# Masks converted one pair after their load, and a first expert layer in fp16 parts

## What is computed

```python
# first attention: 16 heads of 64, mask (4, 1, 512, 512) in int32
energy = jnp.einsum('nqhd,nkhd->nhqk', Qh, Kh) * scale
energy = jnp.where(mask == 0, -1e20, energy)
attention = jax.nn.softmax(energy, axis=-1)
x = x + concat @ Wo
# first experts: 8 experts, each takes the 256 tokens of highest score out of 2048
y = _layernorm(xf[flat_idx].reshape(k, n, d), ln_gamma, ln_beta)
h = jax.nn.gelu(jnp.einsum('knd,nfd->knf', y, fc1s) + b1s, approximate=True)   # 256 -> 1024
o = jnp.einsum('knf,ndf->knd', h, fc2s) + b2s                                  # 1024 -> 256
out = xf.at[flat_idx].add((o * kept_w[:, :, None]).reshape(k * n, d))
```

## Time and profile before

| | |
|---|---|
| median of three runs | 1164.58 us (1164.51 to 1169.02) |
| profiled execution, time | 1166.58 us |
| profiled execution, span | 1164.8 us |
| PE busy | 1056.6 us (91%) |
| DVE, ACT, POOL busy | 753.1, 672.4, 555.8 us |
| first attention, from the first masked score to the last unit | 18 to 504 us |
| first experts | about 566 to 690 us |

### The profile page before, as it was taken

The page is one execution under the profiler, slowest core; times in us unless marked ns, Lnnn a source line. Parts: engine busy times, 40 slices in busy tenths (PEclk is TensorE's granted clock), DMA queues, the critical chain, the costliest instruction groups (busy, mean ns, idle before and its releaser), DMA issues. The chain is left out here.

```text
span 1164.8 us, 28791 instructions
## 1 busy us (share of the span) xinstructions
PE 1056.6 (91%) x10247; PEld 770.4 (66%) x10248; DVE 753.1 (65%) x2151; ACT 672.4 (58%) x1273; POOL 555.8 (48%) x685
## 2 busy tenths in 40 slices
PE   6998999999999999984799997698988867999996
PEld 3666677767777677674488884344554446888885
DVE  5886887788778877878411116677777774555553
ACT  5887876678668876856422235366766643343331
POOL 4677643656556653301436640666667523233312
PEclk9999999999999999995799999899999967999998
DMA  7533333333343334308646546424435231111110
GB/s 258 160 81 82 87 78 75 68 80 82 67 100 92 79 78 92 74 11 294 194 132 181 173 82 221 143 62 141 130 117 152 76 104 37 29 28 30 28 14 11
DMA packets 124380, 117.22 MB, mean 101 GB/s; under 512 B 47840, under 2 KB 104416, under 8 KB 124128
## 3 DMA queue, kind: packets, MB, share of 16 engines
q1 hardware_dynamic: 116960, 106.32, 32.5%
q0 software_dynamic: 7296, 9.25, 4.6%
HBM read 59.89 MB, written 21.82 MB: 70 GB/s over the span
## 5 line engine op out<-in xcount | busy, mean ns | idle before, releaser
L704 ACT ACTIVATE e<-masked,neg_max 128x512 f32<-128x512 f32 x256 | 184.3, 720 | 47.0 <-DVE neg_max L836 43.8
L810 DVE TENSOR_TENSOR e_t_lo<-et,e_t_hi 128x512 f16<-128x512 f32 x256 | 176.6, 690 | 46.0 <-ACT e_t_hi L697 44.0
L836 DVE CUSTOM_DVE_ANT_0 masked<-sc,mask_bias 128x512 f32<-128x512 f32 x256 | 175.5, 686 | 31.2 <-issue 26.9
L697 ACT ACTIVATE e_t_hi<-et 128x512 f16<-128x512 f32 x256 | 151.4, 591 | 69.6 <-PE et L581 68.5
L581 PEld LDWEIGHTS et<-ident,e 128*128 128x128 f32 x1024 | 123.3, 140 | 60.4 <-issue 12.9
L581 PE MATMUL et<-ident,e 128*128 128x128 f32 x1024 | 154.8, 274 | 1.5 <-ACT e L704 0.8
L2260 ACT ACTIVATE d_e<-d_st 128x384 f32<-128x384 f32 (+1 forms) x192 | 93.9, 526 | 49.7 <-PE d_st L2403 45.2
L74 PE MATMUL ob<-v_hi,e_t_hi 128*128 128x65 f16 x1024 | 119.0, 193 | 1.2 <-issue 1.2
L75 PE MATMUL ob<-v_lo,e_t_hi 128*128 128x65 f16 x1024 | 119.2, 193 | 0.0
L76 PE MATMUL ob<-v_hi,e_t_lo 128*128 128x65 f16 x1024 | 118.4, 193 | 0.0
L573 PE MATMUL sc<-kk,qq 128*128 128x512 f16 x254 | 96.1, 378 | 6.1 <-DVE neg_max L836 3.6
(11 more groups left out here) (496 smaller groups left out, 2755.4 us busy)
## 6 DMA issues: line engine op xcount, KB each, us to landing
kk<-nat_k SPq DMA_DIRECT2D x64, 256.0 KB, 3.5
raw<-in_fc SPq DMA_DIRECT2D x16, 1024.0 KB, 7.7
qq<-nat_q SPq DMA_DIRECT2D x64, 128.0 KB, 2.7
qk<-scratch_stack SPq DMA_DIRECT2D x64, 128.0 KB
scratch_stack<-kq_hi SPq DMA_DIRECT2D x16, 256.0 KB, 3.1
scratch_stack<-kq_lo SPq DMA_DIRECT2D x16, 256.0 KB, 3.3
d_expert_raw<-in_gate_w SPq DMA_DIRECT2D x8, 512.0 KB, 3.8
d_expert_raw<-in_up_w SPq DMA_DIRECT2D x8, 512.0 KB, 4.1
```

Of the source, the lines that this page charges most:

```text
L697: nc.scalar.activation(e_t[u % NBUF].hi[:], et[u % 2][:], ACT.Copy).then_inc(turned_hi, 1)
L704: nc.scalar.activation(e[u % NBUF][:], masked[u % NBUF][:], ACT.Exp, bias=neg_max[:, g % 2, j:j + 1], scale=-1.0).then_inc(exp_ok, 1)
L810: nc.vector.tensor_tensor(e_t[u % NBUF].lo[:], et[u % 2][:], e_t[u % NBUF].hi[:], ALU.subtract).then_inc(turned_lo, 1)
L836: nc.vector.tensor_tensor_reduce(masked[u % NBUF][:], sc[j % 2][:], mask_bias[g // PAIRS % 2][:, j % QT, :], -SCALE0, 3e38, ALU.add, ALU.m ...
```

## The change

In the first attention, `bias` is called one pair later than the load of its mask (pairs 4 to 7), and `newton_rounds("z")` moves from pair 3, unit 6 to pair 4, unit 3.

In the first experts, the first layer takes `three_products` of `fc1_parts` and `yt_parts`. ACT makes the high parts (`turned_high`, `weights_high`), DVE the low ones (`turned_low`, `weights_low`); those of the weights of expert e + 2 are made in expert e, so `fc1` is loaded as soon as the low parts of expert e - 2 are made. The weights of experts 0 and 1 are split ahead of the key parts. `wb2` has three buffers for two, and POOL clears the stacks before the scatter instead of behind it.

```diff
-    if (p, j) == (3, 6) and b + 1 in LATE_OF["z"]:
+    if (p, j) == (4, 3) and b + 1 in LATE_OF["z"]:
         return "z", b + 1
...
-                        if j == 2 and g // PAIRS + 1 < B and 0 <= g % PAIRS - MASK_PAIR < QT:
-                            bias((g // PAIRS + 1) * QT + g % PAIRS - MASK_PAIR)
+                        if j == 2 and g // PAIRS + 1 < B and 0 <= g % PAIRS - MASK_PAIR - 1 < QT:
+                            bias((g // PAIRS + 1) * QT + g % PAIRS - MASK_PAIR - 1)
...
+        WB0 = 3
+        yt_parts, fc1_parts = [Split(sb, f"yt{i}", [P, DT, CAP]) for i in range(2)], [Split(sb, f"fc1_{i}", [P, DT, FF0]) for i in range(2)]
-        wb2 = [sb(f"wb2_{i}", [P, HALVES, D]) for i in range(2)]
+        wb2 = [sb(f"wb2_{i}", [P, HALVES, D]) for i in range(WB0)]
...
+                def load_first(e):
+                    sp.wait_ge(fc1_lo, DT * (e - 1))
+                    W.load1(sp, dram, e)
+
+                load_first(2)
+                load_first(3)
                 for e in range(2, E):
-                    sp.wait_ge(h_full, GR * (e - 1))
-                    W.load1(sp, dram, e)
                     sp.wait_ge(fc2_done, HALVES * (e - 1))
                     W.load2(sp, dram, e)
+                    if e + 2 < E:
+                        load_first(e + 2)
...
-                    if e >= 2:
-                        pool.wait_ge(res_ok, HALVES * (e - 1))
+                    if e >= WB0:
+                        pool.wait_ge(res_ok, HALVES * (e - WB0 + 1))
...
-                    if e >= 1:
-                        scatter(e - 1, range(HALVES))
                     if 1 <= e <= QBUF:
                         clear_stacks(e - 1)
                     if e == QBUF + 1:
                         fill_constants()
+                    if e >= 1:
+                        scatter(e - 1, range(HALVES))
...
+                def turned_high(e):
+                    act.wait_ge(affine, e + 1)
+                    if e >= 2:
+                        act.wait_ge(h_full, GR * (e - 1))
+                    nc.scalar.activation(yt_parts[e % 2].hi[:], yt[e % 2][:], ACT.Copy).then_inc(yt_hi, 1)
+
+                def weights_high(e):
+                    act.wait_ge(W.fc1_in[e % 2], 16 * (e // 2 + 1))
+                    if e >= 2:
+                        act.wait_ge(h_full, GR * (e - 1))
+                    for c in range(DT):
+                        nc.scalar.activation(fc1_parts[e % 2].hi[:, c, :], W.fc1[e % 2][:, c, :], ACT.Copy).then_inc(fc1_hi, 1)
+
+                weights_high(0)
+                weights_high(1)
                 for n in range(KEYS_ROUTE, KEYS_FIRST):
...
+                turned_high(0)
                 for e in range(E):
...
+                    if e + 1 < E:
+                        turned_high(e + 1)
+                    if e + 2 < E:
+                        weights_high(e + 2)
                 project.scalar(act)
...
+                def turned_low(e):
+                    dve.wait_ge(yt_hi, e + 1)
+                    nc.vector.tensor_tensor(yt_parts[e % 2].lo[:], yt[e % 2][:], yt_parts[e % 2].hi[:], ALU.subtract).then_inc(yt_lo, 1)
+
+                def weights_low(e):
+                    for c in range(DT):
+                        dve.wait_ge(fc1_hi, DT * e + c + 1)
+                        nc.vector.tensor_tensor(fc1_parts[e % 2].lo[:, c, :], W.fc1[e % 2][:, c, :], fc1_parts[e % 2].hi[:, c, :], ALU.subtract).then_inc(fc1_lo, 1)
+
+                weights_low(0)
+                weights_low(1)
                 for n in range(KEYS_ROUTE, KEYS_FIRST):
...
                 scale_turned(0)
+                turned_low(0)
                 for e in range(E):
                     if e + 1 < E:
                         scale_turned(e + 1)
+                        turned_low(e + 1)
+                    if e + 2 < E:
+                        weights_low(e + 2)
                     if e >= 1:
                         weigh(e - 1)
...
                 def first_layer(e):
-                    pe.wait_ge(W.fc1_in[e % 2], 16 * (e // 2 + 1))
-                    pe.wait_ge(affine, e + 1)
+                    pe.wait_ge(yt_lo, e + 1)
+                    pe.wait_ge(fc1_lo, DT * (e + 1))
...
-                                mm = pe.matmul(hb[n % 2][:, i, :], W.fc1[e % 2][:, c, f * P:(f + 1) * P], yt[e % 2][:, c, :], start=(c == 0), stop=(c == DT - 1))
+                                cols = slice(f * P, (f + 1) * P)
+                                mm = three_products(pe, hb[n % 2][:, i, :], (fc1_parts[e % 2].hi[:, c, cols], fc1_parts[e % 2].lo[:, c, cols]),
+                                                    (yt_parts[e % 2].hi[:, c, :], yt_parts[e % 2].lo[:, c, :]), c == 0, c == DT - 1)
```

More of the change, by code:

```diff
@@ L1539, in phase_experts0 @@
         keys_full, consts = sem("fkeys_full"), sem("fconsts")
+        yt_hi, yt_lo, fc1_hi, fc1_lo = (sem("f" + n) for n in ("yt_hi", "yt_lo", "fc1_hi", "fc1_lo"))
         gathered = [sem(f"fgathered{i}") for i in range(2)]
@@ L1574, in weigh_bias @@
                     pool.tensor_copy(T.slot_weight[:, e, :], yg[e % 2][:, :, D + e]).then_inc(weight_ok, 1)
-                    if e >= 2:
-                        pool.wait_ge(res_ok, HALVES * (e - 1))
+                    if e >= WB0:
+                        pool.wait_ge(res_ok, HALVES * (e - WB0 + 1))
                     pool.wait_ge(weight_ok, e + 1)
                     for n in range(HALVES):
-                        op = pool.tensor_scalar(wb2[e % 2][:, n, :], W.bias2[:, e, :], T.slot_weight[:, e, n:n + 1], None, ALU.mult)
+                        op = pool.tensor_scalar(wb2[e % WB0][:, n, :], W.bias2[:, e, :], T.slot_weight[:, e, n:n + 1], None, ALU.mult)
                     op.then_inc(wb2_ok, 1)
@@ L1660, in weigh @@
                         nc.vector.scalar_tensor_tensor(out=res[e % 2][:, n, :], in0=ob[e % 2][n], scalar=T.slot_weight[:, e, n:n + 1],
-                                                            in1=wb2[e % 2][:, n, :], op0=ALU.mult, op1=ALU.add).then_inc(res_ok, 1)
+                                                            in1=wb2[e % WB0][:, n, :], op0=ALU.mult, op1=ALU.add).then_inc(res_ok, 1)
+                def turned_low(e):
[7 more added lines that the diff above has]
+                weights_low(1)
                 for n in range(KEYS_ROUTE, KEYS_FIRST):
```

## The result

The changed kernel takes 1147.52 us (1145.65 to 1148.94, 4 runs) beside 1164.55 (1162.11 to 1169.02, 4 runs) of the kernel before: a ratio of 0.9855, 95% interval 0.9825 to 0.9885. The profiled execution took 1146.52 us, where the prediction's sum makes 1155.0.

What follows compares the result with a forecast made beforehand. TensorE (PE) was taken as the bound. Gains of 4.3 (attention) and 9.0 (experts) less 1.7 (clock) made 11.6 us, taking the profiled 1166.58 to 1155.0, median 1153.0; range 1148.5 to 1160.

Steps and rivals of the forecast that it cites:

- the attention term: First attention: removing POOL's mask waits gains only PE's holes, 4.3 us, bounds 2.5 and 5.6.
- (5): Rival: no clock fall and all attention holes closed, so 1150 us or a little under; chance 0.08.
- The clock's term: Start of first experts: one spell of half clock loses 1.7 us, bounds 0 and 5.1.
- The hole of 1.0 us: Expert 0's third group on PE waits for the first gelu with its table load, 1.0 instead of 0.54.
- 12.58 per expert: First experts: fp16 products in the first layer cut each expert from 14.26 to 12.58 us.
- 11.66 for 11.76 behind the start: First experts: seven experts behind the first save 1.68 us each, 11.76 us.
- first layers late: Start of first experts: first layers of experts 0 and 1 begin 2.2 and 2.7 us later.
- pair 4 at 14.65: First attention, batch 0: pair 4 would take near 15.0 us and not 17.32.
- DVE's wait in pair 5: First attention, batch 0: DVE's normalisation in pair 5 still waits about 2 us for POOL.
- rival 2: First experts: gelu table reload at every change between Copy and Gelu, 8 us back, 1161; chance 0.04.
- Rival (4): First experts: late weight loads hold back gelus on ACT once landing over 12.0 us after issue; slower; chance 0.06.
- rival 3: First experts: POOL becomes the bound, held up by DVE's new differences, 10 us back, 1163; chance 0.06.

Runs made afterwards that it cites:

- kernel 5: Kernel before the change with only the mask loads issued one pair earlier, conversions and newton_rounds left in place: 1152.76 us, ratio 0.9915.
- 1: Kernel before plus only the attention part of the change (conversions a pair later, newton_rounds in pair 4): 1153.28 us, ratio 0.9917.
- 3: Kernel before with only the mask conversions moved a pair later, newton_rounds left in pair 3: 1155.25 us, ratio 0.9931.
- Kernel 2: Kernel before plus only the experts part of the change: 1156.53 us, ratio 0.9927.
- kernel 8: Changed kernel with two wb2 buffers and the scatter ahead of the clearing again, as before the change: 1152.14 us, ratio 0.9907.
- Kernel 11: Changed kernel run once more without any edit: 1146.51 us, ratio 0.9864.
- 12: Changed kernel, newton_rounds back in pair 3, expert 1's weights split behind the key parts, ACT converting turned rows ahead of the gelus for expert 1 alone: 1142.77 us.
- 7: Changed kernel with newton_rounds back in pair 3 and expert 1's weights split behind the key parts and turned_high(0): 1142.65 us, ratio 0.9829.

## Why the prediction was off

**The step that failed is the attention term: "Worth: only PE's holes", 4.3 with an upper bound of 5.6; measured 9.2 to 9.4.** Of it 4.32 are batch 0 (125.64 to 121.32 us) where I had 2.50, and 4.86 batches 1 and 2 where I had 1.8. The mechanism, POOL's waits for the masks, was right, as kernel 5 shows; its size was read from the wrong column. Windows of pairs 5 and 6 of batch 1 in the kernel before, and below them the same pairs in the changed kernel, cut from first masked score to first masked score:

```profile
223.17:240.47 17.30, 16.38 (x174) 10.89 (x172) 13.61 (x44) 12.56 (x23) 10.26 (x10) 1.00 0.31 77
240.47:256.65 16.18, 15.80 (x181) 11.07 (x180) 13.17 (x44) 13.09 (x24) 10.53 (x13) 1.00 0.42 83
```
```profile
218.67:234.38 15.71, 15.71 (x174) 10.91 (x172) 13.61 (x45) 12.56 (x23) 10.24 (x11) 1.00 0.35 86
234.38:248.53 14.15, 14.15 (x167) 10.36 (x166) 12.30 (x44) 12.54 (x23) 8.89 (x9) 1.00 0.37 94
```

The holes before are 0.92 and 0.38 us; the pairs became 1.59 and 2.03 shorter, and in the first, with 174 records in both, PE's busy time fell by 0.67. A single place in the kernel before (PE's timeline):

```profile
236.62 0.19 PE L74 MATMUL ob<-v_hi,e_t_hi 128*128 128x65 f16 x1
...
236.95 0.19 PE L76 MATMUL ob<-v_hi,e_t_lo 128*128 128x65 f16 x1
237.33 0.38 PE L573 MATMUL sc<-kk,qq 128*128 128x512 f16 x1 [0.18 <-DVE neg_max L836]
```

The `ob` products start each 0.03 us, so the next score could start at about 236.98; in the changed kernel it does, 0.36 us behind the first of them (231.10 to 231.46), here 0.71. The profile calls 0.18 of these 0.35 us idle, because the last record is drawn 0.19 long. By the same rows I estimate that a wait under about 0.16 us (0.19 - 0.03) would show nothing. A delay that reaches PE in many such pieces is in no hole.

A part of the size stood in another column, DVE's waits for POOL in the kernel before:

```profile
228.34 0.18 DVE L819 RECIPROCAL rden<-ob 128x4 f32<-128x4 f32 x1 [1.65 <-POOL o_parts L393]
352.70 0.18 DVE L819 RECIPROCAL rden<-ob 128x4 f32<-128x4 f32 x1 [0.70 <-POOL o_parts L393]
```

They lie in pair 5 of batches 1 and 2, and these pairs became 1.59 and 0.65 us shorter. In batch 0 the waits of 2.21 and 1.25 in pairs 5 and 6 became 1.66 and none, the pairs 0.55 and 1.18 shorter. With pair 4's 2.67 that is 6.64 of the 9.2. The rest is pair 6 of batches 1 and 2 (2.03 and 0.80 shorter, less 0.3 by which the last pairs became longer), where DVE shows no such wait; how the delay got there was not traced.

The length of a pair against that of the same pair without the delay would have shown it: batch 1 stood there with 125.31 us beside 123.13 for batch 2, the same work, 2.2 us apart. Even the shorter one was delayed: without the waits (the changed kernel, 1, 3 and 5) both batches take 121.8. Which pair is hit differs from one execution to the next. Kernel 2 has the attention of the kernel before, and its batch 1 takes 122.79 and its batch 0, from pair 3 on, 80.79 for 78.29 (there with a slice at half clock, 98.5 to 102.0); the sum hardly moves (stage A 427.01 for 426.42).

Of the rivals (5), with a chance of 0.08, came nearest: 1150 or a little under, by more from both stages. It too had attention bounded by its holes, at 5.6.

**The clock's term was too high: 1.7, of which at most 0.5 reached the stage.** The spell came, one slice long, in expert 0 (a window, and under it ACT's timeline; changed kernel):

```profile
566.97:570.38 3.41, 2.77 (x14) 1.91 (x15) 1.49 (x3) 1.16 (x1) 3.07 (x4) 0.50 1.03 278
566.85 1.28 ACT L1665 ACT_TABLE_LOAD   x1
```

The 48 products of expert 0's first layer start from 567.61 to 574.09 without a hole, the first 13 of them 0.213 us apart and the rest 0.109. That is 6.48 us where 47 x 0.109 are 5.12, so PE lost 1.35 us to the clock. Two things kept this out of the sum. The hole of 1.0 us that I had put before the third group never came, since the table load was over at 568.13 and the first gelu, at 570.39, waited for PE. And the turning ahead of expert 1's first layer waited until 575.62 for its gathered rows (its row is above). At full clock, then, the layer could by my estimate have started at 575.62 + 0.44 = 576.06, only 0.48 ahead of its 576.54. The 2.86 us of lateness so are 2.4 and at most 0.5, where I had 2.7 and 1.7. A fall during the key products is in both kernels (it ends 5.8 us behind `r_slot_bank` before, 5.3 after) and makes no difference between them.

A second slice did cost something: in kernels 2 and 8, of those with the new experts the only ones with two in this layer, expert 1 starts 1.77 and 1.58 us later than in the changed kernel. Kernel 11, the changed kernel again, had one, and its expert 1 starts at 21.65 for 21.69. Its stage E kept 8.4 us of the 8.8; the 0.4 are a later turning, at 639.09, that waited for gathered rows.

**The rest, 1.8 us.** 0.54 in routing and 1.30 behind the last `res` were not in the sum, and no edit touches them. The same code behind the last `res` took 471.0 us in kernel 8, 473.3 in kernel 11 (the changed kernel again), 475.5 in 12 and 477.7 in 7, so they are within what one execution differs from the next. With 5.1 from attention and 1.5 from the experts they are the 8.5 us between 1155.0 and 1146.52.

**What held.** 0.109 us from product to product, 12.58 per expert, 11.66 for 11.76 behind the start; first layers late by 2.08 and 2.86 for 2.2 and 2.7 (the second by luck in part, since it holds the clock's share); pair 4 at 14.65 (I said near 15.0), DVE's wait in pair 5 1.66 (about 2); one table load (rival 2 fell). Rival (4) stayed away with little to spare: the load issued at 589.30 held ACT until 599.85, 10.55 us, where I had 8 and put the limit at 12.0. ACT then stood 1.44 us idle before its next gelu at 603.29, so the limit in this expert is 11.99. (My own terms, 8 and 3.5 us of cover, make 11.5.)

```profile
599.85 2.00 ACT L1648 ACTIVATE fc_hi<-raw 128x1024 f16<-128x1024 f32 x2 [3.92 <-DMA raw<-in_fc]
```

**POOL (rival 3).** It didn't become the bound in the changed kernel. But I gave the third `wb2` buffer and the new order no price, only a sentence, and kernel 8 gives them one: 4.5 us of stage E behind expert 1's start, 4.6 by the medians of the time. Without them the new work of DVE would have brought about half of rival (3)'s 10 us by another way than I had in mind: not by the sum of POOL's work, but by its queue. And where DVE's differences do meet POOL, POOL is held (changed kernel, timeline):

```profile
558.09 2.01 POOL L1578 DMA_INDIRECT yg<-scratch_y,slot_token  x1 [0.30 <-issue]
560.39 1.94 POOL L1578 DMA_INDIRECT yg<-scratch_y,slot_token  x1 [0.30 <-issue]
...
575.91 3.89 POOL L1588 TENSOR_SCALAR wb<-bias,slot_weight 128x256 f32<-128x256 f32 x2
```

The product (two instructions) takes 1.83 us alone, the gather 0.95 to 1.0. The 3.89 lie beside two differences of DVE from 576.73 to 579.09. The rule of the Trainium skill that the prediction weighed (SBUF — State Buffer, "SBUF: two separate sides") has a DVE instruction with two SBUF inputs and a GpSimd instruction that reads SBUF shut each other out. For POOL the trace agrees with that rule; for DVE it doesn't show it, since the two differences took 1.23 and 1.22 us, as they do alone. It cost nothing in the steady state, where POOL still waits for `res` between its jobs (5.31 us at 604.50).

## What to carry to other kernels

A gap in PE's busy time was here a lower bound of what a delay cost it: compare the length of a repeated unit with the same unit undisturbed, and count short waits at their distance from start to start. Before moving a job on an in-order queue, ask what its producer itself stands behind: the same move was worth 1.3 us of stage for one expert and cost 4.6 to 6.1 when made for all. A buffer, or an order, that looks like a by-product of a change can be what keeps its new work off the path, so it deserves its own term. Two losses at the start of a stage need not add: one can lie under the other, as the clock's 1.35 us lay under a wait for gathered rows. And where a load can be issued earlier (kernel 5), that is as good as moving its user.

## What the runs showed of the hardware that was not expected

PE's records of 65-column products overlap the next start by some 0.16 us (0.19 us drawn, 0.03 us pace), which hides waits. POOL's indirect gathers, which work on addresses, took 2.01 and 1.94 us beside DVE's two-input differences for 0.95 to 1.0 without them, as its arithmetic did (3.89 for 1.83), while DVE's differences kept their 1.22 us. The clock's fall in expert 0's first layer was one slice long in the changed kernel (twice) and two in kernels 2 and 8, whose code from the key products to that layer is the same on PE, ACT and DVE; the second slice goes with an expert 1 that starts 1.6 to 1.8 us later.
